# Bilinear hats loaded by one transfer per image, and the residual written by GpSimd: a change to a deformable convolution kernel

## What is computed

```python
def _bilinear_sample(x, py, px):
    y0, x0 = jnp.floor(py), jnp.floor(px)
    for dy in (0.0, 1.0):
        for dx in (0.0, 1.0):
            yi, xi = y0 + dy, x0 + dx
            wy = 1.0 - jnp.abs(py - yi)
            wx = 1.0 - jnp.abs(px - xi)
            ...
            out = out + v * (wy * wx * valid.astype(x.dtype))[None]
    return out
...
def _block(x, dc_w, dc_b, of_w, of_b, dw, db):
    h = jax.nn.relu(_deconv2d(x, dc_w, dc_b))
    offset = _conv2d(h, of_w, of_b, PAD)
    return jax.nn.relu(_deform_conv2d(h, offset, dw, db))
...
for i in range(1, 4):
    in_cur = x + in_prev
    x = _block(in_cur, deconv_w[i], ...)
    in_prev = in_cur
x_cat = jnp.concatenate((x, in_module), axis=1)
offset = _conv2d(x_cat, fin_off_w, fin_off_b, PAD)
return _deform_conv2d(x_cat, offset, fin_dcn_w, fin_dcn_b)
```

## Times and profile before

| | us |
|---|---|
| median of 3 runs | 4395.29 (4390.24 to 4401.12) |
| the profiled execution | 4397.31 |
| its span, first to last instruction | 4395.5 |
| PE busy | 3411.8 (78%) |
| DVE busy | 3105.5 (71%) |
| ACT busy | 2412.1 (55%) |
| GpSimd (POOL) busy | 1549.7 (35%) |
| mean granted TensorE clock | 0.903 of full speed |

### The profile page before, as it was taken

The page is one execution under the profiler, slowest core; times in us unless marked ns, Lnnn a source line. Parts: engine busy times, 40 slices in busy tenths (PEclk is TensorE's granted clock), DMA queues, the critical chain, the costliest instruction groups (busy, mean ns, idle before and its releaser), DMA issues.

```text
span 4395.5 us, 199600 instructions
## 1 busy us (share of the span) xinstructions
PE 3411.8 (78%) x71156; PEld 2425.1 (55%) x71156; DVE 3105.5 (71%) x5798; ACT 2412.1 (55%) x6331; POOL 1549.7 (35%) x805
## 2 busy tenths in 40 slices
PE   4788588588758858876876886788588888588887
PEld 3555465355536645554554554455366666366665
DVE  5785688588578758856866885786576675476665
ACT  1775377277447727745763773676155554155554
POOL 1552354155245425514532551453222221222221
PEclk8898799799979979987997998799799999799999
DMA  4442544344254334425434443443766664666664
GB/s 137 120 127 73 143 125 119 85 125 126 68 153 124 108 99 125 128 76 142 125 95 111 127 128 81 133 124 104 178 160 153 158 153 108 172 161 150 156 157 110
DMA packets 329328, 554.66 MB, mean 126 GB/s; under 512 B 145680, under 2 KB 236048, under 8 KB 311696
## 3 DMA queue, kind: packets, MB, share of 16 engines
q1 hardware_dynamic: 235184, 498.90, 42.6%
q10 hardware_dynamic: 93760, 50.87, 4.3%
HBM read 472.10 MB, written 77.42 MB: 125 GB/s over the span
## 4 chain that ended last, share of the span: by engine, by line
SPq 38%; PE 31%; issue 13%; ACT 7%; DVE 7%; DMA 2%; POOLq 0%; ACTq 0%; DVEq 0%; PEld 0%; PEldq 0%
SPq L420 19%; SPq L404 17%; PE PS L605 16%; PE P L549 7%; PE PS L618 5%; ACT SMP L783 4%; PE P L578 2%; DVE A L964 1%; ACT YC L799 1%; DVE ST L1078 1%; DVE FOFF L1075 1%; DVE YC L1084 1%; DMA VT<-ht_store 1%; PE PS L549 1%; ACT H L891 1%
## 5 line engine op out<-in xcount | busy, mean ns | idle before, releaser
L964 DVE TENSOR_TENSOR A<-P,YC 121x384 f32<-121x384 f32 (+1 forms) x4608 | 2285.1, 550 | 796.6 <-ACT YC L799 742.2
L799 ACT ACTIVATE YC<-P 121x384 f32<-121x384 f32 (+1 forms) x4608 | 1706.8, 445 | 416.7 <-PE P L578 374.1
L605 PE MATMUL PS<-A,VT 121*32 121x80 f32 (+1 forms) x40960 | 1398.0, 258 | 436.0 <-DMA VT<-ht_store 258.7
L605 PEld LDWEIGHTS PS<-A,VT 121*32 121x32 f32 (+1 forms) x40960 | 1142.7, 122 | 741.2 <-issue 334.2
L1168 POOL TENSOR_SCALAR CLIP<-HB,CONST 128x2304 int16<-128x2304 int16 x320 | 722.2, 2257 | 1873.5 <-PE P L578 1712.0
L578 PE MATMUL P<-HL,SEL 32*121 32x384 f16 (+1 forms) x10752 | 1169.8, 324 | 177.8 <-issue 95.0
L783 ACT ACTIVATE SMP<-PS 128x480 f32<-128x480 f32 (+3 forms) x1152 | 594.7, 516 | 837.4 <-PE PS L605 831.8
L578 PEld LDWEIGHTS P<-HL,SEL 32*121 32x121 f16 (+1 forms) x10752 | 517.4, 118 | 645.8 <-issue 232.8
L1170 POOL TENSOR_SCALAR HL<-CLIP,CONST 128x2304 f16<-128x2304 int16 x320 | 724.2, 2263 | 66.2 <-POOL CLIP L1168 66.2
L618 PE MATMUL PS<-SMP,CW 128*64 128x128 f32 x7424 | 495.2, 284 | 13.4 <-ACT SMP L783 6.7
L958 DVE SCALAR_TENSOR_TENSOR X<-X,CONST,TMP 128x128 f32 (+1 forms) x320 | 408.3, 1276 | 79.2 <-ACT TMP L771 79.2
(11 more groups left out here) (65 smaller groups left out, 890.9 us busy)
## 6 DMA issues: line engine op xcount, KB each, us to landing
HB<-part_store SPq DMA_DIRECT2D x2560, 72.0 KB
VT<-ht_store SPq DMA_DIRECT2D x256, 512.0 KB
VT<-ht_store SPq DMA_DIRECT2D x768, 132.0 KB
VT<-ht_store SPq DMA_DIRECT2D x256, 88.0 KB
off_store<-FOFF ACTq DMA_DIRECT2D x160, 128.0 KB, 3.0
part_store<-FPART SPq DMA_DIRECT2D x160, 128.0 KB, 2.9
H<-x_dram SPq DMA_DIRECT2D x5, 2048.0 KB, 15.7
ht_store<-A ACTq DMA_DIRECT2D x32, 256.0 KB, 3.2
```

The lines of the kernel that those rows point to most:

```text
L605: mm = nc.tensor.matmul(PS[q:q + wide, sh.unit * v:sh.unit * (v + 1)].rearrange("p (k y x) -> p k y x", k=sh.taps, y=BLK), vt[:, img, :], ...
L799: nc.scalar.activation(YC[0:sh.npos, g % X_SLOTS, 0:sh.size], P[0:sh.npos, g % Y_SLOTS, 0:sh.size], ACT.Copy, scale=1.0 / UNIT).then_inc(y ...
L964: return nc.vector.tensor_tensor(dst, x, y, ALU.mult)
```

## The change

1. In `HB`, a quadrant's 32 rows now alternate high, low, high, low, instead of 16 high and 16 low ones. One transfer with a source pattern of 16 repeats x 2 parts x 2304 numbers fills an image's 32 partitions, so `load_offsets` issues 4 transfers instead of 8. The semaphore's counts are halved with it (`HB_LOAD`), and `_tables` follows the new order of rows.
2. The residual leaves DVE. GpSimd does it in two passes: X times `FLAGS` (a tile that DVE fills once per layer with the layer's flag), a wait, then plus `TMP`. It stands after the hats of a chunk, one chunk later than before; the last two or three follow at the end of the step.
3. In the final layer GpSimd waits for `x_back`, ahead of the hats of chunk 2; DVE no longer does.
4. `MINUS` is laid over a part of `SMP`, which frees the room for `FLAGS`.

```diff
+HB_LOAD = IMG * 16
...
-        MINUS = sb("MINUS", [128, 2, 128])
+        FLAGS = sb("FLAGS", [128, CPX])
...
+        MINUS = SMP[:, 1, 0:256].rearrange("p (a b) -> p a b", a=2)
...
                 for i in range(IMG):
-                    for part in range(2):
-                        at = band * W_BAND + (i * BANDS * 4 + 2 * part + half) * CH * CPX
-                        src = bass.AP(part_store.ap().tensor, at, [[0, AXIS], [1, HAT]])
-                        q = CH * i + AXIS * part
-                        sp.dma_start(HB[q:q + AXIS, half, :], src).then_inc(hb_full[half], 16)
+                    at = (i * BANDS + band) * W_BAND + half * CH * CPX
+                    src = bass.AP(part_store.ap().tensor, at, [[0, AXIS], [2 * CH * CPX, 2], [1, HAT]])
+                    sp.dma_start(HB[CH * i:CH * (i + 1), half, :], src).then_inc(hb_full[half], 16)
...
+                flag = CONST[:, LAYERS:LAYERS + 1] if final else CONST[:, bass.ds(layer, 1)]
+                nc.vector.tensor_copy(FLAGS[:, :], flag.broadcast_to([128, CPX]))
...
-                            if before >= sh.lag and b == sh.batches - 1 and g == sh.sum_after + 2:
-                                if sh.lag == 2:
-                                    add_residual(c - 2, band - 1, half)
-                                else:
-                                    add_residual(c - 1, band + half - 1, 1 - half)
...
-                def input_back(c, band, half, before, last):
-                    body(c, band, half, before, last)
-                    if final and before == 0:
-
-                        dve.wait_ge(x_back, 16 * group + 16)
...
-            def body_of(sh):
-                def body(c, band, half, before, last):
-                    if before > 0:
+            def body_of(sh, layer, group, final):
+                def add_residual(c, band, half):
+
+                    if final:
+                        dst = out_view(group, BLK * band, COLS * half, COLS)
+                    else:
+                        dst = x_view(group, BLK * band, COLS * half, BLK, COLS)
+                    flags = FLAGS[:, :].rearrange("p (r c) -> p r c", r=BLK)
+                    wait_alone(pool, ps_free, (c + 1) * sh.ps_uses + 1)
+                    nc.gpsimd.tensor_tensor(dst, dst, flags, ALU.mult).then_inc(kept_step, 1)
+                    wait_alone(pool, kept_step, c + 1)
+                    nc.gpsimd.tensor_tensor(dst, dst, TMP[:, half, :].rearrange("p (r c) -> p r c", r=BLK),
+                                            ALU.add).then_inc(res_done, 1)
+
+                def body(c, band, half, start=2):
+                    if start > 0:
 
                         wait_alone(pool, x_full, (c - 1) * sh.batches * sh.ngr + 1)
                         hats(c, band, half)
-
-                chunk_loop(pool, body, lambda: None)
+                    if start > sh.lag:
+
+                        if sh.lag == 2:
+                            add_residual(c - 3, band - 2 + half, 1 - half)
+                        else:
+                            add_residual(c - 2, band - 1, half)
+
+                for c in range(4):
+                    if final and c == sh.lag + 1:
+
+                        wait_alone(pool, x_back, 16 * group + 16)
+                    body(c, c // 2, c % 2, c)
...
+                for c in range(CHUNKS - 1 - sh.lag, CHUNKS):
+                    add_residual(c, c // 2, c % 2)
...
-    q = row % AXIS
-    low_part = row >= AXIS
+    q = row // 2
+    low_part = row % 2 == 1
```

More of the change, by code:

```diff
@@ L203, in build @@
         clip_done = sem("clip_done")
+        kept_step = sem("kept_step")
         hats_full = sem("hats_full")
@@ L215, in build @@
                     coarse_done, fine_done, parts_ready, *off_stored, *far_stored, far_full, range_done,
-                    flag_step, *hb_full, clip_done, hats_full, y_full, y_ready, x_full, product_done,
+                    flag_step, *hb_full, clip_done, kept_step, hats_full, y_full, y_ready, x_full, product_done,
                     *vt_full, ps_full, ps_free, res_done, turn]
@@ L465, in fallback @@
                         if half == 0:
-                            sp.wait_ge(hb_full[0], 2 * 32 * IMG)
-                            sp.wait_ge(hb_full[1], 32 * IMG)
+                            sp.wait_ge(hb_full[0], 2 * HB_LOAD)
+                            sp.wait_ge(hb_full[1], HB_LOAD)
                             for slot in range(OFF_SLOTS):
@@ L947, in layer_start, with residual @@
                 wait_alone(dve, bias_step, 2 * layer + 2)
-            def residual(layer, group, band, half, final, tmp=None):
-                src = TMP[:, half if tmp is None else tmp, :].rearrange("p (r c) -> p r c", r=BLK)
+                flag = CONST[:, LAYERS:LAYERS + 1] if final else CONST[:, bass.ds(layer, 1)]
+                nc.vector.tensor_copy(FLAGS[:, :], flag.broadcast_to([128, CPX]))
+            def residual(layer, group, band, half, final, tmp):
+                src = TMP[:, tmp, :].rearrange("p (r c) -> p r c", r=BLK)
                 if final:
@@ L974, in one_product @@
                     return product(sh, a[:, :, at:at + sh.size], x, YC[0:sh.npos, g % X_SLOTS:g % X_SLOTS + 1, 0:sh.size])
-                def add_residual(c, band, half):
-                    dve.wait_ge(ps_free, (c + 1) * sh.ps_uses + 1)
-                    residual(layer, group, band, half, final).then_inc(res_done, 1)
                 def body(c, band, half, before, last):
@@ L993, in body @@
                             one_product(g, b, half).then_inc(product_done, 1)
-                            if before >= sh.lag and b == sh.batches - 1 and g == sh.sum_after + 2:
-                                if sh.lag == 2:
-                                    add_residual(c - 2, band - 1, half)
-                                else:
-                                    add_residual(c - 1, band + half - 1, 1 - half)
[L1000 to L1003, removed]
-                def input_back(c, band, half, before, last):
-                    body(c, band, half, before, last)
-                    if final and before == 0:
-                        dve.wait_ge(x_back, 16 * group + 16)
-                chunk_loop(dve, input_back, tail)
+                chunk_loop(dve, body, lambda: None)
             def fallback_of(sh, layer, group, final):
@@ L1163, in hats @@
             def hats(c, band, half, wait_clip=True):
-                wait_alone(pool, hb_full[half], 32 * IMG * (band + 1))
+                wait_alone(pool, hb_full[half], HB_LOAD * (band + 1))
                 if wait_clip:
@@ L1186, in split @@
                                         ALU.mult).then_inc(whole_done, 1)
-            def body_of(sh):
-                def body(c, band, half, before, last):
-                    if before > 0:
+            def body_of(sh, layer, group, final):
[12 more added lines that the diff above has]
+                    if start > 0:
                         wait_alone(pool, x_full, (c - 1) * sh.batches * sh.ngr + 1)
                         hats(c, band, half)
-                chunk_loop(pool, body, lambda: None)
+                    if start > sh.lag:
[7 more added lines that the diff above has]
+                    body(c, c // 2, c % 2, c)
+                with pool.Fori(0, BANDS - 3) as pair:
+                    body(2 * pair + 4, pair + 2, 0, 4)
+                    body(2 * pair + 5, pair + 2, 1, 4)
+                body(CHUNKS - 2, BANDS - 1, 0, 4)
+                body(CHUNKS - 1, BANDS - 1, 1, 4)
+                for c in range(CHUNKS - 1 - sh.lag, CHUNKS):
+                    add_residual(c, c // 2, c % 2)
             def step(layer, group, bar_count, final):
@@ L1200, in step @@
                 hats(0, 0, 0, wait_clip=False)
-                sampling(pool, bar_count, final, body_of, lambda sh: None, clears=True)
+                sampling(pool, bar_count, final, lambda sh: body_of(sh, layer, group, final), lambda sh: None, clears=True)
             each_step(pool, lambda layer, final: None, step, clears=True)
@@ L1208, in _tables @@
     row = np.arange(128) % 32
-    q = row % AXIS
-    low_part = row >= AXIS
+    q = row // 2
+    low_part = row % 2 == 1
+    last = q == AXIS - 1
     is_x = row >= AXIS
-    last = q == AXIS - 1
+    far_q = row % AXIS
     rel = np.full((128, 2, 2, 128), 99.0, np.float32)
@@ L1226, in _tables @@
                 sel[:, table, first + n] = (q == (at - 1) % AXIS) * 1.0 - (~last & (q == at))
-            sel[:, 5 + tile, first + n] = (is_x & (q == j + LANES * (n % columns))) / SCALE
-            sel[:, 7, first + n] = (~is_x & (q == n // columns)) / SCALE
+            sel[:, 5 + tile, first + n] = (is_x & (far_q == j + LANES * (n % columns))) / SCALE
+            sel[:, 7, first + n] = (~is_x & (far_q == n // columns)) / SCALE
     pxc = np.zeros((STRIPES, CH, STRIPE_ROWS, COLS), np.float32)
@@ L1234, in _tables @@
     consts[:, 0:5] = [0.0, 1.0, 1.0, 0.0, 1.0]
-    consts[:, 5] = SCALE * (MARGIN - q)
```

(3 more changed lines are left out.)

## The result

The changed kernel takes 4126.6 us (median of 4 runs, 4119.5 to 4130.3), before 4394.2 us in the same comparison: a ratio of 0.939, 95% interval 0.937 to 0.941. The forecast was 4101, the range 4000 to 4190. The span of the profiled execution is 4128.2 us.

A forecast was written before the change was run, and what follows sets the result against it. SP's issuing queue was taken as the bound. Savings of 257 (loop), 27 (step starts) and 16 (wait for X), less 6 (tails), made 294 us off the profiled 4397.3: 4103, or 4101 by the median; range 4000 to 4190.

The forecast's parts named there:

- SP's queue is the bound, and stays it: Ordinary steps: SP's issuing sets the pace, 8.55 us a chunk before and 7.44 after, narrowly behind which comes ACT - PE.
- Issue time of the new transfer: HB loads on SP's queue: 0.54 us per new instruction, bounds 0.316 and 0.832; a group of four takes 2.73 us.
- The loop's gain: HB groups in the eight ordinary steps: 1.11 us saved on each of 29 groups a step, 257 us in all.
- The chain behind it at 7.17: ACT and PE in ordinary steps: without the residual on DVE their chain could go at 7.17 us a chunk.
- The start of the step: HB issues ahead of the barrier: three groups save 3.3 us a step, 27 us over eight steps.
- the tails: Ends of ten steps: GpSimd's two exposed passes and a semaphore replace 0.344 us, costing 0.6 us each, 6 us in all.
- The residual leaves DVE: Ordinary steps: DVE's residual waits for GpSimd's HL pass; on GpSimd two passes of 0.4 us each would be hidden.
- near 7.9: Ordinary steps: the chunk time in us expected if the loads changed but the residual stayed on DVE.
- The 7.94 of the earlier trace: Kernel before: ACT's time between two sum reads, in us; less 0.60 and 0.17 it gave 7.17.
- The wait for X: Last layer: moving DVE's wait for the input to GpSimd, ahead of chunk 2's hats, hides it and saves 16 us.

The follow-up runs named there:

- residual_only: The changed kernel with the old row order and 8 HB transfers a group, residual still on GpSimd: 4388.9 us, ratio 0.998 to the kernel before.
- flat_hb: The changed kernel with the part dimension taken out of the HB loads' source pattern, low part not loaded, for measuring alone: 4015.2 us, ratio 0.913.
- pool_queue: The changed kernel with one of four HB transfers of each loop group issued by GpSimd instead of SP: 4051.4 us, ratio 0.921.
- combined: pool_queue with the residual in one pass on DVE after the tenth product, DVE waiting for X only before the last layer's first residual: 4029.3 us.
- loads_only: The kernel before with interleaved rows and 4 HB transfers a group, residual and wait for X left on DVE: 4341.1 us, ratio 0.987.
- late_residual: loads_only with DVE's residual after the tenth product of a chunk instead of the fourth: 4141.8 us, ratio 0.941 to the kernel before.

## Why the prediction was right, point by point

- **SP's queue is the bound, and stays it.** Right; `residual_only` shows it for before, the 0.79 us of PE's wait, `flat_hb` and `pool_queue` for after.
- **Issue time of the new transfer.** 0.54 taken, 0.578 measured, with gaps of 0.20 instead of 0.19. The group is 2.96 us, not 2.73, so the gain is 0.88 us a chunk, not 1.11. This is the term that was mis-sized; it alone makes 0.23 x 29 x 8 = 53 us. The reason that I gave was half right: the form, not the size, makes the price.
- **The loop's gain.** 257 forecast, 231 measured. The issue time would leave 204; the other 27 us nobody had forecast, and that they made up for half of the miss is luck. Most of them come from the first chunks of a step, before SP's steady pace: over the eight steps the first six chunks got 7.6 us shorter, where 0.88 each makes 5.3. In step 1 three groups from 121.21 to 150.37 (29.2 us) now go from 117.83 to 140.84 (23.0), 6.2 us less and not 2.6, which I put down to the HB groups at that place standing between a CLIP and a window load that PE waits for; no run tells it apart.
- **The chain behind it at 7.17.** Observed at 7.21 in `flat_hb`, and at 7.23 in `combined`.
- **The start of the step.** 27 us forecast, 27 measured; PE's 3.4 us in step 1. `loads_only` and `late_residual`, without the two passes, gain 25 in the same stretches, so the tails that were to cost 6 us are not seen there; in `residual_only` these stretches are 3 us longer than before.
- **The residual leaves DVE.** Right that DVE's instruction waited for GpSimd's; right that GpSimd hides two passes: 0.41 to 0.46 us each, 0.4 taken. Too small was what the residual would cost if left: "near 7.9" stood for a chunk without a lapse of the clock, and was 8.55. The 7.94 of the earlier trace rows was one chunk; in that step they run from 6.9 to 11.6 us. The forecast did not need it, but the weight of the two halves did.
- **The wait for X.** This step failed in part. Up to the first sum the last layer gained 19 us, most of it the wait of 16.4, but its loops lost 10. I had asked only whether GpSimd's hats would come in time, and not whether the window load of that chunk would, which stands on SP's queue behind HB issues that are late: here by the wait for X, in `combined` by busy DMA engines. That the two large transfers are what keeps the engines busy is argued from the times; no run leaves them out.

So the sum missed by 27 us: the loops gave 26 less than forecast and the last layer 7 less (19 - 10 = 9 for 16), while the 6 us set down for the tails did not show as a loss of their own.

## What to carry to other kernels

An issuing queue that never waits is a bound like any engine; count its instructions and the time that one holds it, not the bytes. Where two resources have nearly the same period, change both or expect little: here 1.3% and 0.2% apart, 6.1% together. Before moving an instruction to another engine because it is slow, look at what runs beside it; moving it six products later did the same here, and left the other engine free to take over a DMA.

## What the runs showed of the hardware

- Issuing a flat transfer held SP's queue for 0.316 us with 16 rows and with 32; the same bytes with a third dimension 0.578; a 33-row window load 0.81 to 0.83.
- Outer dimension 2 instead of 16 in the source pattern: two packets under way at once instead of up to 16 and more, and 5919 us in place of 4127.
- A DVE instruction of 0.344 us took 1.98 beside a GpSimd pass of 2.26, ending 0.14 us after it.
- Three issues held the queue for 15.9 us while the DMA engines' share was 0.95 (eight for 17.2 in the kernel before, at 0.88); the window load behind them left at 2819.69, when they were through.
- In `loads_only` matmuls ran at nearly half the speed (2.40 us for 1.31, granted clock 0.50) behind a wait of PE of 0.72 us, in a chunk of 10.4 us; in the changed kernel a wait of 0.79 us left the clock at 1.00.
